# Attention block with layer norms, one core: another order of loads and preparation in the prologue, and 44 transposes ahead of the first x

## The reference, cut to what matters

```python
xn = layernorm(x, g_in)                       # over the 512 features
q  = (xn @ Wq) * 64**-0.5                     # 512 -> 16 heads x 64
kv = xn @ Wkv                                 # 512 -> 64 keys + 64 values, one head for all
k, v = concat(null_kv, kv)                    # one null key/value ahead of the 128
sim = q @ k.T + attn_bias                     # (null_attn_bias for the null key)
sim = where(causal | key_mask, -max, sim)
out = softmax(sim) @ v                        # heads joined: 1024
x + layernorm(out @ Wo, g_out)
```

## Time and profile before

| | |
|---|---|
| median of 3 runs | 1103.74 us (1101.32 to 1104.71) |
| the profiled execution | 1105.91 us, span 1103.9 us |
| PE busy | 1035.2 us (94%) |
| PEld, DVE, ACT, POOL busy | 905.5, 769.9, 660.7, 830.2 us |
| chain that ended last, by engine | PE 66%, DVE 9%, issue 8%, POOL 8%, ACT 4% |
| mean granted clock of TensorE | 0.982 |

### The profile page before, as it was taken

One profiled execution on the slowest core, in us unless ns is written; L12 is line 12 of the kernel. 1 busy time (PEld: TensorE's weight loads), 2 busy tenths in 40 slices (PEclk: granted clock), 3 DMA queues, 4 the chain that ended last, 5 costly groups with the idle time before them and its releaser, 6 DMA issues.

```text
span 1103.9 us, 42925 instructions
## 1 busy us (share of the span) xinstructions
PE 1035.2 (94%) x14224; PEld 905.5 (82%) x14224; DVE 769.9 (70%) x3517; ACT 660.7 (60%) x2617; POOL 830.2 (75%) x1488
## 2 busy tenths in 40 slices
PE   4779999999999999999999999999999999999975
PEld 4668888888888888888888888888888888888853
DVE  4667777767777776777777677776767767776551
ACT  4546755656665565666556566656656665665551
POOL 1758787787877778788777878877787887877763
PEclk9889999999999999999999999999999999999987
DMA  7312222221222222222222222222322222221101
GB/s 212 102 44 69 81 83 81 70 88 56 76 84 83 77 77 70 73 79 81 84 74 80 79 59 82 83 82 67 89 69 69 82 83 82 68 69 50 49 22 39
DMA packets 90013, 84.01 MB, mean 76 GB/s; under 512 B 21568, under 2 KB 64064, under 8 KB 89792
## 3 DMA queue, kind: packets, MB, share of 16 engines
q1 hardware_dynamic: 87680, 78.97, 24.0%
q10 hardware_dynamic: 2112, 2.10, 0.6%
HBM read 40.11 MB, written 16.78 MB: 52 GB/s over the span
## 4 chain that ended last, share of the span: by engine, by line
PE 66%; DVE 9%; issue 8%; POOL 8%; ACT 4%; SPq 1%; DVEq 1%; ACTq 0%; POOLq 0%; DMA 0%
PE ps_pv L476 34%; PE ps_proj L482 21%; PE ps_s L439 7%; PE ps_pv L463 5%; POOL bias_b L878 3%; DVE logit_bot L546 2%; ACT exp_bot L749 2%; DVE y_stats L575 2%; POOL small L911 2%; DVE o_lo L567 2%; POOL w_nrm L887 2%; SPq L331 1%; ACT exp_top L749 1%; DVE neg_max L546 1%; ACT o_hi L757 1%
## 5 line engine op out<-in xcount | busy, mean ns | idle before, releaser
L749 ACT ACTIVATE exp_bot<-logit_bot,neg_max 128x129 f32<-128x129 f32 x512 | 201.4, 396 | 314.0 <-DVE neg_max L546 292.2
L482 PE MATMUL ps_proj<-xt_hi,wq_hi 128*128 128x256 f32 x1024 | 303.9, 297 | 4.1 <-DVE q_sb L627 2.6
L878 POOL TENSOR_TENSOR bias_b<-bias_c,mask_add 128x256 f32<-128x256 f32 (+1 forms) x512 | 292.0, 602 | 8.2 <-DVE neg_max L546 7.0
L482 PE MATMUL ps_proj<-xt_hi,wq_lo 128*128 128x256 f32 x1024 | 290.1, 283 | 0.0
L482 PE MATMUL ps_proj<-xt_lo,wq_hi 128*128 128x256 f32 x1024 | 289.9, 283 | 0.0
L546 DVE CUSTOM_DVE_ANT_0 logit_bot<-ps_s,bias_b 128x128 f32<-128x128 f32 x512 | 128.7, 289 | 186.4 <-PE ps_s L439 151.8
L476 PE MATMUL ps_pv<-wo_hi,o_hi 128*128 128x512 f32 x512 | 212.0, 414 | 28.9 <-DVE o_lo L567 28.9
L887 POOL TENSOR_TENSOR w_nrm<-exp_bot,w_inv 128x256 f32<-128x256 f32 x256 | 156.8, 612 | 107.1 <-DVE w_inv L555 107.1
L482 PEld LDWEIGHTS ps_proj<-xt_hi,wq_hi 128*128 128x128 f32 x1024 | 195.0, 190 | 19.1 <-issue 10.5
L476 PE MATMUL ps_pv<-wo_lo,o_hi 128*128 128x512 f32 x512 | 205.6, 402 | 0.0
L476 PE MATMUL ps_pv<-wo_hi,o_lo 128*128 128x512 f32 x512 | 205.3, 401 | 0.0
(11 more groups left out here) (64 smaller groups left out, 1728.0 us busy)
## 6 DMA issues: line engine op xcount, KB each, us to landing
x_in<-in_x_dram SPq DMA_DIRECT2D x32, 512.0 KB, 4.3
x_res<-in_x_dram SPq DMA_DIRECT2D x64, 256.0 KB, 2.8
out_dram<-y_out SPq DMA_DIRECT2D x64, 256.0 KB, 2.1
x_split<-xn SPq DMA_DIRECT2D x480, 32.0 KB, 1.9
v_rep<-v_raw SPq DMA_DIRECT2D x256, 32.0 KB, 1.8
w_raw<-in_L_cond_Wq_dram ACTq DMA_DIRECT2D x4, 512.0 KB, 8.1
w_raw<-in_L_cond_Wo_dram SPq DMA_DIRECT2D x4, 512.0 KB, 5.0
mask_u<-in_mask_BxS_bk_dram SPq DMA_DIRECT2D x32, 32.0 KB, 3.9
```

Of the source, the lines that this page charges most:

```text
L482: mm = pe.matmul(ps[:, 0:TOK], w[:, k, cols], xt[:, slot, k], start=(j == 0), stop=(j == len(todo) - 1))
L749: ins = nc.scalar.activation(out_[:, s, j], in_[:, s, j], ACT.Exp, bias=neg_max[:, s, k:k + 1], scale=-1.0, accum_out=w_sum[:, s, k:k + 1])
L878: ins = nc.gpsimd.tensor_tensor(out_, bias, key_mask, ALU.add)
```

## The change

All of it lies ahead of the loop or in the extras of the first pair.

- TensorE transposes the identity 44 times into PSUM bank `ps_proj[1]` as soon as the identity is made, before it waits for xn.
- SP's queue: x of group 0 in two halves with a semaphore each, Wkv, Wq pieces 0 and 1, the biases, Wq pieces 2 and 3, x and mask of group 1, x and mask of group 2, g_out, Wo. ScalarE's queue has the small ones: g_in (with its own semaphore), null key and value, the mask of group 0.
- The scale of x for groups 0 and 1: epsilon and shift on VectorE (`x_scale_of`), only the power on GpSimd (`x_power_of`). Causal bias and the first masked bias on GpSimd come ahead of group 1's power.
- Wq pieces: ScalarE splits piece 0 behind x 1 (was: ahead of x 0), pieces 1 to 3 behind kv; VectorE takes each quarter of a piece as it comes, piece 0 behind x 1, piece 1 behind q 0, pieces 2 and 3 behind q 3 (was: behind q 1 and q 2). The bias shift moves behind q 1, the statistics of group 1 behind q 3. The mask of group 0 moves behind x 1.
- First pair: statistics of group 2 at step 1 (was 2) on VectorE and GpSimd, `x_norm` at step 2 (was 3); GpSimd's wo_low at steps 3 and 5 (was 1 and 3).

```diff
+WARM = 44
-            load_x(0, 0)
+            sp.dma_start(x_in[:, 0, 0], x_pairs[0, :, 0, :]).then_inc(ld_x[0], 16)
+            sp.dma_start(x_in[:, 0, 1], x_pairs[0, :, 1, :]).then_inc(ld_x_second, 16)
             sp.dma_start(wkv_raw ...).then_inc(ld_wkv, 16)
-            sp.dma_start(gin_col ...); nk_col, nv_col x2; load_mask(0, 0)
+            load_wq(0)
+            load_wq(1)
             ... null bias and bias loads, ten issues ...
+            load_wq(2)
+            load_wq(3)
             load_x(0, 1)
             load_mask(0, 1)
+            load_x_and_mask(1, 0)
             sp.dma_start(gout_row[:], ...)
             ...
-            load_x_and_mask(1, 0)
 # TensorE
             pe.wait_ge(ident_made, 1)
+            for _ in range(WARM):
+                pe.transpose(ps_proj[1][:, 0:P], ident[:], ident[:])
 # VectorE
+            def x_scale_of(f):
+                wait(dve, x_mv_made, GB * f + GB)
+                wait(dve, xn_made, GB * f)
+                nc.vector.tensor_scalar(x_var[:], x_mv[:, :, 1], EPS, None, ALU.add).then_inc(x_var_made, 1)
+                wait(dve, x_rstd_made, f + 1)
+                nc.vector.scalar_tensor_tensor(out=x_shift[:], in0=x_mv[:, :, 0], scalar=minus_one[:, 0:1],
+                                               in1=x_rstd[:], op0=ALU.mult, op1=ALU.mult).then_inc(x_shift_made, 1)
             between = {
-                ("x", 1): lambda: (wq_low(0), wq_low(1)),
-                ("q", 0): lambda: shift_bias(),
-                ("q", 1): lambda: (x_stats_of(0, 1), x_mean_var_of(1), wq_low(2)),
-                ("q", 2): lambda: wq_low(3),
+                ("x", 1): lambda: (mask_of(0, 0), wq_low(0)),
+                ("q", 0): lambda: wq_low(1),
+                ("q", 1): lambda: shift_bias(),
+                ("q", 3): lambda: (wq_low(2), wq_low(3), x_stats_of(0, 1), x_mean_var_of(1), x_scale_of(1)),
             }
             first_extras = {
-                1: lambda: mask_of(1, 1),
-                2: lambda: (x_stats_of(1, 0), x_mean_var_of(BY_PE)),
+                1: lambda: (mask_of(1, 1), x_stats_of(1, 0), x_mean_var_of(BY_PE)),
 # ScalarE
-            for i in range(WP):
-                act.dma_start(raw_piece(i, KT), wq_piece(...)).then_inc(ld_wq[i], 16)
+            act.dma_start(gin_col ...).then_inc(ld_gin, 16); nk_col, nv_col x2, mask_u8[:, 0]
-                ("x", 1): lambda: (wq_high(1), act.wait_ge(shifts_made, 2)),
-                ("kv", 0): lambda: wq_high(2),
-                ("q", 1): lambda: wq_high(3),
+                ("x", 1): lambda: (wq_high(0), act.wait_ge(shifts_made, 2)),
+                ("kv", 0): lambda: (wq_high(1), wq_high(2), wq_high(3)),
                 ("q", 3): lambda: x_norm(1, 1),
-                3: lambda: (x_norm(BY_PE, 0), wo_high(2)),
+                2: lambda: x_norm(BY_PE, 0),
+                3: lambda: wo_high(2),
-            wq_high(0)
 # GpSimd
-            x_rstd_of(0)
+            x_power_of(0)
-            x_rstd_of(1)
-            pool.wait_ge(x_shift_made, 2)
             pool.wait_ge(bias_shifted, 2)
             causal_bias()
             masked_bias(0, 0, 0)
+            x_power_of(1)
             masked_bias(1, 0, 1)
-                1: lambda: wo_low(0),
-                2: lambda: x_rstd_of(BY_PE),
-                3: lambda: wo_low(1),
+                1: lambda: x_rstd_of(BY_PE),
+                3: lambda: wo_low(0),
+                5: lambda: wo_low(1),
```

More of the change, by code:

```diff
@@ L169, in attention_block @@
         ld_cols, ld_rows = sem("ld_cols"), sem("ld_rows")
-        ld_wkv = sem("ld_wkv")
+        ld_wkv, ld_gin, ld_x_second = sem("ld_wkv"), sem("ld_gin"), sem("ld_x_second")
         ld_gout = sem("ld_gout")
@@ L209, in attention_block @@
         y_nrm_made, y_g_made, y_out_made = sem("y_nrm_made"), sem("y_g_made"), sem("y_out_made")
-        COL_LOADS, ROW_LOADS, BIAS_LOADS, V_LOADS = 4, 2, 8, 8
+        COL_LOADS, ROW_LOADS, BIAS_LOADS, V_LOADS = 3, 2, 8, 8
         SPLITS = (N // BLK) * (P // BLK)
@@ L355, in _, with load_wq @@
                 sp.sem_inc(stored[b], 16)
-            load_x(0, 0)
+            sp.dma_start(x_in[:, 0, 0], x_pairs[0, :, 0, :]).then_inc(ld_x[0], 16)
+            sp.dma_start(x_in[:, 0, 1], x_pairs[0, :, 1, :]).then_inc(ld_x_second, 16)
             sp.dma_start(wkv_raw.rearrange("p (k n) -> p k n", k=KT),
                          wkv.rearrange("(k p) n -> p k n", p=P)).then_inc(ld_wkv, 16)
[L359 to L365, removed]
+            def load_wq(i):
+                sp.dma_start(raw_piece(i, KT), wq_piece(wq.rearrange("(k p) n -> p k n", p=P), i)).then_inc(ld_wq[i], 16)
+            load_wq(0)
+            load_wq(1)
             null_by_head = null_bias.rearrange("(c u e) -> u c e", u=2, e=2)
@@ L633, in _ @@
             nc.vector.memset(logit_top[:, :, :, HALF:HALF + 1], 0.0).then_inc(filled, 1)
-            x_stats_of(0, 0)
+            dve.wait_ge(ld_x[0], 16)
+            nc.vector.bn_stats(x_stats[:, 0], x_in[:, 0, 0]).then_inc(x_stat_made, 1)
+            dve.wait_ge(ld_x_second, 16)
+            nc.vector.bn_stats(x_stats[:, 1], x_in[:, 0, 1]).then_inc(x_stat_made, 1)
             x_mean_var_of(0)
-            dve.wait_ge(ld_cols, 16 * COL_LOADS)
-            dve.wait_ge(wkv_hi_made, KT)
+            x_scale_of(0)
+            dve.wait_ge(ld_gin, 16)
             for k in range(KT):
+                dve.wait_ge(wkv_hi_made, k + 1)
                 nc.vector.scalar_tensor_tensor(
@@ L641, in _ @@
                     in1=wkv_hi[:, k].bitcast(F32), op0=ALU.mult, op1=ALU.subtract).then_inc(wkv_lo_made, 1)
+            dve.wait_ge(ld_cols, 16 * COL_LOADS)
             nc.vector.tensor_scalar(k_shift[:], nk_col[:], -SCALE, None, ALU.mult).then_inc(shifts_made, 1)
             nc.vector.tensor_scalar(v_shift[:], nv_col[:], -1.0, None, ALU.mult).then_inc(shifts_made, 1)
-            mask_of(0, 0)
             def wq_low(i):
-                dve.wait_ge(wq_hi_made, KT * (i + 1))
                 for k in range(KT):
+                    dve.wait_ge(wq_hi_made, KT * i + k + 1)
                     nc.vector.scalar_tensor_tensor(
@@ L801, in front @@
                                          bias=v_shift[DH:P, 0:1]).then_inc(v_raw_made, 1)
-            for i in range(WP):
-                act.dma_start(raw_piece(i, KT), wq_piece(wq.rearrange("(k p) n -> p k n", p=P), i)).then_inc(ld_wq[i], 16)
+            act.dma_start(gin_col[:], g_in.rearrange("(k p) -> p k", p=P),
+                          allow_slow_non_contiguous=True).then_inc(ld_gin, 16)
+            act.dma_start(nk_col[:], null_kv[0].rearrange("(d o) -> d o", o=1)).then_inc(ld_cols, 16)
+            for half in range(2):
+                act.dma_start(nv_col[DH * half:DH * (half + 1)],
+                              null_kv[1].rearrange("(d o) -> d o", o=1)).then_inc(ld_cols, 16)
+            act.dma_start(mask_u8[:, 0].rearrange("p b n -> p (b n)"),
+                          mask_pairs[0, 0:TOK].partition_broadcast(P)).then_inc(ld_mask[0], 16)
             x_norm(0, 0)
-            act.wait_ge(ld_cols, 16 * COL_LOADS)
+            act.wait_ge(ld_gin, 16)
             act.wait_ge(ld_wkv, 16)
@@ L901, in x_rstd_of @@
                 nc.gpsimd.tensor_tensor(x_mr[:], x_mv[:, :, 0], x_rstd[:], ALU.mult).then_inc(x_mr_made, 1)
-                wait(pool, x_mr_made, f + 1)
+                wait(pool, x_mr_made, f + 1 - BY_PE)
                 nc.gpsimd.tensor_tensor(x_shift[:], x_mr[:], minus_one[:], ALU.mult).then_inc(x_shift_made, 1)
@@ L933, in _, with x_power_of @@
             pool.wait_ge(filled, 1)
-            x_rstd_of(0)
+            def x_power_of(f):
+                wait(pool, x_var_made, f + 1)
+                wait(pool, xn_made, GB * f)
+                nc.gpsimd.tensor_tensor(x_rstd[:], x_var[:], pow_col[:], ALU.pow).then_inc(x_rstd_made, 1)
+            x_power_of(0)
             def causal_bias():
```

## The result

The changed kernel takes 1115.83 us (median of 4 runs, 1112.49 to 1117.18) against 1104.17 for the kernel before in the same session (4 runs): ratio 1.0106, 95% interval 1.0077 to 1.0136. The forecast was 1094.2, range 1089.5 to 1099. The profiled execution took 1116.74 us with a span of 1114.8 (before 1105.91 and 1103.9).

What follows compares the result with a forecast made beforehand. TensorE, busy 97.87 of 100 us in the loop, bounds the kernel, so only the start can shrink: group 2's xn 11.5 us earlier, less 2.0 for the clock, gives 1103.7 - 9.5 = 1094.2 us; range 1089.5 to 1099.

Steps and rivals of the forecast that it cites:

- The step that failed: Whole kernel: a prologue shorter by d makes the kernel shorter by d, since no wait is on an absolute time.
- the price of the transposes: TensorE's start: 44 identity transposes at most 0.22 us each, ending at 11.2, taken as hidden, at worst 1.5 us.
- prediction's signs of being wrong: Profile after: x after 6, ScalarE waiting for Wq 2 or 3, wo_low last before projection, or loop's TensorE share dropping.
- x in halves, statistics, xn: Group 0's start: second half of x lands at 4.5 instead of 6.27, xn ends at 8.2 instead of 11.13.
- rival C: Prologue: clock falls before KV, so KV and Q0 to Q3 run slow; shift 7.0, 1096.7 us; chance 0.14.
- Weights one at a time: Prologue, Wq pieces: pieces 2 and 3 no longer precede the scores, which begin at 20.3 instead of 30.51.
- Rival D: Prologue: Wq pieces 2 and 3 come late in SP's queue; shift 7.2, 1096.5 us; chance 0.08.
- Rival A: The forecast itself: clock low over Q6 after the idle gap; shift 9.5, 1094.2 us; chance 0.46.
- B: Gap before Q6 leaves the clock up; shift 11.5, 1092.2 us; chance 0.22.
- the term of 2.0 us: Q6, Q7 and transposes behind TensorE's 3.2 us gap: low clock costs 2.0 us, between 0 and 3.4.
- rival E: First pair, step 5: GpSimd becomes last before batch 0's output projection, making the kernel slower; 1106.6 us at 72; chance 0.06.
- All four faster cases: Cases A to D, shifts of 7.0 to 11.5 us, 1092.2 to 1096.7 us; together 0.90.

Runs made afterwards that it cites:

- kernel 2: The kernel before with the 44 identity transposes alone, written out ahead of its prologue; 1115.28 us, ratio 1.011.
- kernel 4: The kernel before with 44 small 32x32 transposes on TensorE ahead of step 0, no early start; 1120.49 us, ratio 1.0129.
- kernel 1: The changed kernel without its 44 transposes (WARM = 0); 1104.12 us, ratio 1.0001.
- kernel 5: kernel 3 with 8 short instructions more at VectorE's start; 1098.75 us, ratio 0.995.
- kernel 6: The kernel before with 5 short instructions more at VectorE's start; 1109.21 us, ratio 1.0042.
- kernel 3: The changed kernel with 84 small transposes more on TensorE ahead of step 1 of the first pair; 1101.0 us, ratio 0.9968.
- kernel 7: The changed kernel with 40 small transposes more ahead of the loop; 1150.77 us, ratio 1.0423.
- kernel 13: The changed kernel with 10 small transposes more ahead of the loop; 1138.81 us, ratio 1.0302, two runs only.
- kernel 14: The changed kernel with 20 small transposes more ahead of the loop; 1140.77 us, ratio 1.032, two runs only.
- kernel 15: The changed kernel with 63 small transposes more ahead of the loop; 1103.07 us, ratio 0.9971.
- kernel 8: The changed kernel with its 44 transposes as a loop of 11 times 4, plus 8 short VectorE instructions; 1099.13 us, ratio 0.9959.
- kernel 9: kernel 8 with 14 loop rounds instead of 11 (56 transposes); median not in the text, forecast of 1095 to 1096 missed.
- kernel 12: kernel 9 with a loop of 24 more identity transposes in TensorE's gap before Q6; 0.48% under the kernel before.
- kernel 10: The changed kernel without transposes, with 8 short instructions more at VectorE's start; worth 4.5 us against the kernel before.

## Why the prediction was wrong

**The step that failed** is in its first paragraph: "whatever moves the first pairs' end by some us moves the end of the kernel by as many: every wait in it is on another engine, none on an absolute time. A kernel whose prologue is shorter by d is shorter by d." Kernels 2 and 4 show it false: the waits of the loop depend on the length of the code ahead of it too. For the same reason the price of the transposes was wrong in kind. I costed 44 by the time they take and hid them under x's landing; they took 7.96 us and were as good as hidden. Their price was 88 places in TensorE's code, a term that the sum did not have: 14.6 us of periods (the changed kernel against kernel 1). VectorE's 5 instructions, which I had priced as statistics and scales, cost another 4 (18.8 against 15.0 in kernel 1, with kernels 5 and 6 for the cause). Of the prediction's signs of being wrong the last one came: the loop's TensorE share dropped, from 97.87 to 96.85 of 100 us. The profile could have warned: it lists the instruction queues, and `values` and scores issue 80 and 32 matmuls in 1.6 and 0.9 us.

**x in halves, statistics, xn.** Forecast 8.2 for the end of xn, measured 7.57 + 1.52 = 9.09. The second half landed by 5.18, when its statistics began, not at 4.5; the rest is handovers.

**Transposes, K and V.** KV at 12.20 (forecast 11.6) at full clock: rival C did not come in this trace. That was partly luck. Kernels 3, 5, 7, 13, 14 and 15 run the same 44 transposes, and TensorE's code is the same up to the scores; in all of them but kernel 3 the transposes ended at 8.2 to 8.9 instead of 9.1 to 9.5, the clock fell to 0.50 between 11.8 and 13.3, and the scores came at 22.8 to 23.0 instead of 21.5. C's price is 1.3 to 1.5 us by that, and 1.85 at the first projection by kernels 8 and 9, where I had given it 2.5.

**Weights one at a time.** Scores at 21.50 (20.3); this step carried most of the gain, as forecast. Rival D was there in part: ScalarE waited 1.51 us for Wq piece 2, and nothing for piece 3.
```profile
18.66 1.71 ACT L838 ACTIVATE wq_hi<-w_raw,small 128x256 fp32r<-128x256 f32 x4 [1.51 <-DMA w_raw<-in_L_cond_Wq_dram]
```
**The gap and the clock.** Gap 3.52 before Q6 (3.2), clock 0.50 behind it for 3.4 us, as behind the gaps of the earlier trace rows. Rival A over B was right, and the term of 2.0 us is measured by kernel 12 as 2.19. Kernels 7 and 15 agree: they had no stretch of 0.50 from 30 to 35 us and xn of group 2 at 44.1, against 45.7 to 46.5 in kernels 5, 13 and 14, which had one and whose scores came at the same time.

**Sum of the start.** xn of group 2 ended at 44.19 instead of 43.4, x_split's chain then took 12.2 us (12.4). Shift 8.86 against 9.5, in one trace; the other six kernels with this prologue had the first projection at 60.5 to 64.1, so one trace fixes this number only to some 2 us. wo_low 1 on GpSimd (2.34 us) ended at 58.03, before the projection at 60.23; rival E did not decide.

**The range and the chances.** All four faster cases rested on the failed step, and so did rival E. That slower could come from outside the prologue had 0.07 together with E. With both codes on a free place the order gives 4.5 us (kernel 10), and 5.8 with clock and gap seen to (kernel 12): less than the 5.0 and 8.5 by which their first projections are early. Part of that is the end of the kernel, which took 63.2 to 65.1 us from its last pair's first projection in these traces, with its own low stretches of the clock.

## What to carry to other kernels

When an edit puts instructions ahead of a hardware loop with a long body, compare the loop's period before and after first, and look for waits on "issue" in the middle of a run of equal instructions: they are a matter of where the code lies, not of what it does. Filler work belongs into a short hardware loop (11 rounds of 4 moved nothing), and a change of a few us is judged at two or three offsets of the code, since small transposes that moved the code and computed nothing took this kernel from 1101 to 1151 us. An idle gap that brings the clock down is worth filling where what follows is on the path: 24 transposes gave 2.2 us at the first projection.

## What the hardware showed that was not expected

- A halt at a code boundary was 0.4 to 3.0 us of idle time and came back in every round that was entered by the jump back, never in the first. Behind some of them the granted clock was 0.50, mostly for 3.4 us: three times in the changed kernel, ten times in kernel 7 with its halts of 2.5.
- Transposes written out once, outside the loop, cost more inside it (14.6 us) than they took (7.96).
- Whether 44 of them kept the clock up until K and V differed from kernel to kernel with the same code up to there: in two of seven traces they did.
- On VectorE the same kind of shift by 5 short instructions was 0.36 us a pair, and 8 made the loop as short as before.
